# Ten first products from a constant, a pair copy and the placing of blocks off GpSimd, and the constants by two transfers

## The reference, cut to what matters

```python
# x [32, 32, 256], subjects [32] of 8, bias [8, 32], cond weights [8, 32, 32]
h = einsum('bct,bcd->bdt', x, weights[subjects]) + bias[subjects][:, :, None]
# the FFN runs over the last axis of h (256), hidden size 768; w.astype(float8) is the quantization
gate = silu((h @ q(gate_w)) * gate_scale)
up   = (h @ q(up_w)) * up_scale
out  = x + ((gate * up) @ q(down_w)) * down_scale
```

## Time and profile before

| | |
|---|---|
| median of 3 runs | 49.52 us (49.23 to 49.99) |
| the profiled execution, whole | 49.15 us |
| its span in the profile | 47.4 us |
| TensorE busy | 42.6 us (90%) |
| VectorE busy | 38.1 us (81%) |
| ScalarE busy | 25.2 us (53%) |
| GpSimd busy | 4.4 us (9%) |

### The profile page before, as it was taken

How to read it: one execution, slowest core, us unless ns; L and a number is a source line. 1 busy time by engine, 2 the same in 40 slices (tenths; PEclk the granted TensorE clock), 3 DMA queues, 4 the chain that set the end, 5 groups by cost and what they waited for, 6 DMA issues and landing times.

```text
span 47.4 us, 664 instructions
## 1 busy us (share of the span) xinstructions
PE 42.6 (90%) x201; PEld 33.4 (70%) x201; DVE 38.1 (81%) x70; ACT 25.2 (53%) x43; POOL 4.4 (9%) x13
## 2 busy tenths in 40 slices
PE   1999899999999999999999999999999999999000
PEld 1332498798788888888888888887888898987000
DVE  2838899998999999999999999958455569995900
ACT  3734257847519895988695609046554647430000
POOL 3028585200000000000000000000000000000000
PEclk9999999999999999999999999999999999999998
DMA  0398999999990000000000000000000000034392
GB/s 0 99 341 306 353 373 395 404 407 412 417 384 21 0 0 0 14 0 0 0 0 0 0 7 0 0 0 0 0 0 0 0 0 0 7 133 189 121 347 96
DMA packets 2851, 5.71 MB, mean 121 GB/s; under 512 B 288, under 2 KB 928, under 8 KB 2848
## 3 DMA queue, kind: packets, MB, share of 16 engines
q1 hardware_dynamic: 2704, 5.55, 31.6%
q10 hardware_dynamic: 144, 0.13, 0.8%
HBM read 4.63 MB, written 1.05 MB: 120 GB/s over the span
## 4 chain that ended last, share of the span: by engine, by line
PE 73%; DVE 10%; DMA 5%; POOL 2%; issue 2%; ACT 1%; DVEq 1%; POOLq 0%
PE gu L505 46%; PE acc L513 23%; DVE tree_sb L373 6%; DMA const_in<-in_consts_dram 5%; PE acc L478 4%; DVE res L418 2%; POOL cond_bd L314 2%; ACT tree_sb L223 1%; DVEq L70 1%; DVE cond_bd L380 1%; DVEq L364 0%; DVEq L378 0%; POOLq L312 0%
## 5 line engine op out<-in xcount | busy, mean ns | idle before, releaser
L505 PE MATMUL gu<-h_hi,w_q 128*128 128x512 f32 (+1 forms) x52 | 15.0, 376 | 0.0
L505 PE MATMUL gu<-h_lo,w_q 128*128 128x512 f32 (+1 forms) x52 | 14.9, 374 | 0.0
L260 ACT CAST f_hi<-fuse 128x512 fp32r<-128x512 f32 (+1 forms) x13 | 7.6, 588 | 8.8 <-DVE fuse L405 8.6
L505 PEld LDWEIGHTS gu<-h_hi,w_q 128*128 128x128 f32 x52 | 9.5, 188 | 1.9
L505 PEld LDWEIGHTS gu<-h_lo,w_q 128*128 128x128 f32 x52 | 9.5, 188 | 1.8
L405 DVE SCALAR_TENSOR_TENSOR fuse<-gu,const_in,silu 128x512 f32<-128x512 f32 (+1 forms) x13 | 9.2, 706 | 1.5 <-PE gu L505 1.1
L253 ACT ACTIVATE silu<-gu,const_in 128x512 f32<-128x512 f32 (+1 forms) x13 | 8.5, 654 | 3.3 <-PE gu L505 3.3
L413 DVE TENSOR_TENSOR f_lo<-fuse,f_hi 128x512 fp32r<-128x512 f32 (+1 forms) x13 | 8.3, 646 | 2.1 <-ACT f_hi L260 2.1
L513 PE MATMUL acc<-f_lo,w_q 128*128 128x512 f32 (+1 forms) x26 | 8.3, 378 | 0.0
L513 PE MATMUL acc<-f_hi,w_q 128*128 128x512 f32 (+1 forms) x26 | 8.2, 374 | 0.0
L335 DVE SCALAR_TENSOR_TENSOR w_q<-w_big,w_in 128x768 fp32r<-128x768 f32 (+2 forms) x8 | 6.0, 754 | 0.1
(11 more groups left out here) (28 smaller groups left out, 15.9 us busy)
## 6 DMA issues: line engine op xcount, KB each, us to landing
w_in<-in_weights_dram SPq DMA_DIRECT2D x4, 384.0 KB, 6.0
x_tok<-in_x_by_time_dram SPq DMA_DIRECT2D x1, 1024.0 KB, 8.7
out_dram<-res SPq DMA_DIRECT2D x3, 256.0 KB, 2.0
x_sb<-in_x_dram SPq DMA_DIRECT2D x1, 512.0 KB, 3.6
w_in<-in_weights_dram SPq DMA_DIRECT2D x2, 256.0 KB, 4.5
x_sb<-in_x_dram SPq DMA_DIRECT2D x2, 256.0 KB, 4.7
w_in<-in_weights_dram SPq DMA_DIRECT2D x2, 128.0 KB, 5.0
const_in<-in_consts_dram SPq DMA_DIRECT2D x1, 171.0 KB, 2.3
```

Source lines behind the costliest of these rows:

```text
L260: nc.scalar.copy(f_hi[:, s % SLOTS, cols], fuse[:, s % SLOTS, cols]).then_inc(f_hi_made, 1)
L505: last = nc.tensor.matmul(gu[:, (s + q) % 2, part, cols], w_q[:, i, col:col + P], h[:, n, k, cols], start=(v == 0 and k == 0), stop=(v == ...
```

## The change

Four edits. TensorE's first products read a constant of ones in bf16 that the program makes for itself ahead of the kernel's block, broadcast along both dimensions, in place of `warm`; they wait for nothing, there are ten of them and not nine, and VectorE's memset L338 is gone. The copy of the fourth pair of half 0 goes from GpSimd to VectorE, behind the bits and ahead of `select(0)`. The placing goes off GpSimd: in both halves ScalarE places j = 0 and 1, and VectorE j = 2 and 3; GpSimd keeps only the bias work, with both `bias_tok` products in a row. And `const_in` comes by two transfers of 64 partitions each, the first issued by SP as its first, the second by ScalarE ahead of its table load, both counting on `const_ld`, for which everyone now waits to reach 32.

```diff
--- before.py
+++ after.py
@@ -9,7 +9,6 @@
 F32 = mybir.dt.float32
 F32R = mybir.dt.float32r
 I32 = mybir.dt.int32
-U32 = mybir.dt.uint32
 
 P = 128
 
@@ -42,7 +41,7 @@
 
     LAST = 2
     LO_ROW = 32
-    WARM = 9
+    WARM = 10
 
     PIECES = [slice(q * TOK // LAST, (q + 1) * TOK // LAST) for q in range(LAST)]
 
@@ -90,7 +89,6 @@
         w_q = sb("w_q", [P, IC, WCOL], F32R)
         bit_of = sb("bit_of", [P, BITS], I32)
         iota_p = sb("iota_p", [P, 1])
-        warm = sb("warm", [P, P], BF16)
         ones_f = sb("ones_f", [P, P])
         ones_r = sb("ones_r", [P, P], F32R)
         pick_b = sb("pick_b", [P, B])
@@ -111,6 +109,7 @@
         gu = ps("gu", [P, 2, 2, 512])
 
         warm_ps = gu[:, 0, 0]
+        ones_b = nc.const_aps.tensor(1.0, [P, TOK], BF16)
         tree = [tree_sb[:, n].rearrange("p (q g d) -> p q g d", g=GH, d=D) for n in range(HALVES)]
         bits_ps = gu[:, 0, 1, 0:BITS * G].bitcast(I32).rearrange("p (k g) -> p k g", g=G)
 
@@ -119,7 +118,6 @@
         x_ld = [[sem("x_ld0")], [sem(f"x_ld1_{k}") for k in range(KC)]]
         w_ld = [sem(f"w_ld{i}") for i in range(IC)]
         w_down_ld = [sem(f"w_down_ld{i}") for i in range(2)]
-        warm_set = sem("warm_set")
         iota_made = sem("iota_made")
         ones_set = sem("ones_set")
         bit_set = sem("bit_set")
@@ -127,7 +125,7 @@
         bits_made = sem("bits_made")
         bias_pick_made = sem("bias_pick_made")
         tree_even = [sem(f"tree_even{n}") for n in range(HALVES)]
-        tree_even_pool = sem("tree_even_pool")
+        tree_even_dve = sem("tree_even_dve")
         tree_level = [sem(f"tree_level{n}") for n in range(HALVES)]
         cond_placed = [sem(f"cond_placed{n}") for n in range(HALVES)]
         bias_hi_made = sem("bias_hi_made")
@@ -157,9 +155,7 @@
 
         QUANT = ((0, 0, GU), (1, 0, GU), (0, GU, WCOL), (2, 0, WCOL), (1, GU, WCOL)) + tuple((i, 0, WCOL) for i in range(3, IC))
 
-        ACT_BLOCKS = ((0,), (0,))
-        POOL_BLOCKS = ((1,), (1, 2))
-        DVE_BLOCKS = ((2, 3), (3,))
+        ACT_BLOCKS, DVE_BLOCKS = (0, 1), (2, 3)
 
         def wait_quant(eng, i, lo):
 
@@ -184,7 +180,7 @@
             def load_w(i):
                 sp.dma_start(w_in[:, i], weights[i]).then_inc(w_ld[i], 16)
 
-            sp.dma_start(const_in[:], consts).then_inc(const_ld, 16)
+            sp.dma_start(const_in[0:P // 2], consts[0:P // 2]).then_inc(const_ld, 16)
             sp.dma_start(x_sb[:, 0], x[0].rearrange("k p g t -> p k g t")).then_inc(x_ld[0][0], 16)
             load_gate_up(0)
             load_x(0)
@@ -217,9 +213,10 @@
                 act.wait_ge(w_down_ld[i] if lo == GU else w_ld[i], 16)
                 nc.scalar.activation(w_big[:, i, lo:hi], w_in[:, i, lo:hi], ACT.Abs, scale=SHIFT).then_inc(quant_big, 1)
 
+            act.dma_start(const_in[P // 2:P], consts[P // 2:P]).then_inc(const_ld, 16)
             nc.scalar.preload_act_table(ACT.Silu)
 
-            act.wait_ge(const_ld, 16)
+            act.wait_ge(const_ld, 32)
             nc.scalar.copy(tree[0][:, 0:PAIRS - 1], cond_rep[:, 0:PAIRS - 1, 0].unsqueeze(2).to_broadcast([P, PAIRS - 1, GH, D])
                            ).then_inc(tree_even[0], 1)
             nc.scalar.copy(tree[1], cond_rep[:, :, 0].unsqueeze(2).to_broadcast([P, PAIRS, GH, D])
@@ -227,7 +224,7 @@
 
             def place(n):
                 act.wait_ge(tree_level[n], BITS)
-                for j in ACT_BLOCKS[n]:
+                for j in ACT_BLOCKS:
                     nc.scalar.copy(*block_of(n, j)).then_inc(cond_placed[n], 1)
 
             def high_of_h(n, k):
@@ -285,12 +282,6 @@
                            allow_small_or_imprecise_dtypes=True).then_inc(iota_made, 1)
             pool.wait_ge(iota_made, 2)
 
-
-            pool.wait_ge(const_ld, 16)
-            nc.gpsimd.tensor_copy(tree[0][:, PAIRS - 1], cond_rep[:, PAIRS - 1, 0].unsqueeze(1).to_broadcast([P, GH, D])
-                                  ).then_inc(tree_even_pool, 1)
-            pool.wait_ge(tree_even_pool, 1)
-
             def place_bias(n):
 
                 batches = slice(n * TOK // D, (n + 1) * TOK // D)
@@ -307,19 +298,7 @@
             pool.wait_ge(bias_lo_made, 1)
             place_bias(0)
 
-            def place(n):
-
-                pool.wait_ge(tree_level[n], BITS)
-                for j in POOL_BLOCKS[n]:
-                    nc.gpsimd.tensor_copy(*block_of(n, j)).then_inc(cond_placed[n], 1)
-                pool.wait_ge(cond_placed[n], J)
-
-            pool.wait_ge(bd_zeroed, 1)
-            pool.wait_ge(bias_placed, 1)
-            place(0)
             place_bias(1)
-            pool.wait_ge(bias_placed, 2)
-            place(1)
 
         @block.vector
         def _(dve):
@@ -335,7 +314,6 @@
                 nc.vector.scalar_tensor_tensor(w_q[:, i, lo:hi], w_big[:, i, lo:hi], LEAST, w_in[:, i, lo:hi],
                                                ALU.max, ALU.subtract).then_inc(quant_made, 1)
 
-            nc.vector.memset(warm[:].bitcast(U32), 0).then_inc(warm_set, 1)
             nc.vector.memset(ones_f[:], 1.0).then_inc(ones_set, 1)
             for k in range(BITS):
                 nc.vector.memset(bit_of[:, k:k + 1], 1 << k).then_inc(bit_set, 1)
@@ -345,7 +323,7 @@
 
 
 
-            dve.wait_ge(const_ld, 16)
+            dve.wait_ge(const_ld, 32)
             nc.vector.tensor_copy(bias_r[:], bias_in).then_inc(bias_hi_made, 1)
             dve.wait_ge(iota_made, 2)
             nc.vector.tensor_tensor(pick_b[:], subj_all, iota_p[:].to_broadcast([P, B]), ALU.is_equal).then_inc(bias_pick_made, 1)
@@ -353,6 +331,8 @@
             nc.vector.tensor_tensor(bits_ps, subj_own.unsqueeze(1).to_broadcast([P, BITS, G]),
                                     bit_of[:].unsqueeze(2).to_broadcast([P, BITS, G]),
                                     ALU.bitwise_and).then_inc(bits_made, 1)
+            nc.vector.tensor_copy(tree[0][:, PAIRS - 1], cond_rep[:, PAIRS - 1, 0].unsqueeze(1).to_broadcast([P, GH, D])
+                                  ).then_inc(tree_even_dve, 1)
 
             def select(n):
 
@@ -361,7 +341,7 @@
                     left = PAIRS >> k
                     if k == 0:
                         dve.wait_ge(tree_even[n], 1)
-                        dve.wait_ge(tree_even_pool, 1)
+                        dve.wait_ge(tree_even_dve, 1)
                         to = tree[n]
                         data = cond_rep[:, :, 1].unsqueeze(2).to_broadcast([P, PAIRS, GH, D])
                     else:
@@ -372,12 +352,15 @@
                     mask = bits_ps[:, k, groups].unsqueeze(1).unsqueeze(3).to_broadcast([P, left, GH, D])
                     nc.vector.copy_predicated(to, mask, data).then_inc(tree_level[n], 1)
 
+            def place(n):
+                dve.wait_ge(tree_level[n], BITS)
+                for j in DVE_BLOCKS:
+                    nc.vector.tensor_copy(*block_of(n, j)).then_inc(cond_placed[n], 1)
+
+            dve.wait_ge(bd_zeroed, 1)
             dve.wait_ge(bits_made, 1)
             select(0)
-            dve.wait_ge(bd_zeroed, 1)
-            dve.wait_ge(tree_level[0], BITS)
-            for j in DVE_BLOCKS[0]:
-                nc.vector.tensor_copy(*block_of(0, j)).then_inc(cond_placed[0], 1)
+            place(0)
             select(1)
 
             def rest_of_h(n, k):
@@ -385,9 +368,7 @@
                 nc.vector.tensor_tensor(h_lo[:, n, k], acc[:, KC * n + k], h_hi[:, n, k].bitcast(F32),
                                         ALU.subtract).then_inc(h_lo_made, 1)
 
-            dve.wait_ge(tree_level[1], BITS)
-            for j in DVE_BLOCKS[1]:
-                nc.vector.tensor_copy(*block_of(1, j)).then_inc(cond_placed[1], 1)
+            place(1)
             rest_of_w(0)
             round_w(0)
             for n in range(HALVES):
@@ -459,7 +440,7 @@
         def _(pe):
             def keep_warm(count):
                 for _ in range(count):
-                    nc.tensor.matmul(warm_ps, warm[:], warm[:].unsqueeze(1).to_broadcast([P, TOK // P, P]), start=True, stop=True)
+                    nc.tensor.matmul(warm_ps, ones_b[:, 0:P], ones_b, start=True, stop=True)
 
             def bias_of(n):
 
@@ -480,7 +461,6 @@
                                                 start=False, stop=(g == GH - 1), skip_group_check=True)
                     last.then_inc(h_made, 1)
 
-            pe.wait_ge(warm_set, 1)
             keep_warm(WARM)
             for n in range(HALVES):
                 bias_of(n)
```

## The result

The changed kernel took 50.14 us (median of 4 runs, 49.59 to 51.72) where the kernel before took 49.47 in the same series (4 runs, 49.23 to 49.99): a ratio of 1.0134, with a 95% interval of 1.0094 to 1.0175. In a second series, beside 29 runs of the kernel before, it was 1.0138 (1.0089 to 1.0186). So it is slower by 0.7 us, which is under 2 per cent, with an interval that leaves out no change, where 0.37 us less was forecast. The ratios leave out executions more than 1.5 per cent above the fastest of the same kernel, the medians don't.

A forecast was written before the change was run, and what follows sets the result against it. A prologue until 8.61 us, then TensorE alone, bound the kernel, so only an earlier `condition(1)` pays. 0.02 + 0.35 = 0.37 us off 49.52 gave 49.15, called 49.1 us (forecast 48.9 to 49.3, chance 0.48); range 48.5 to 49.8.

The forecast's parts named there:

- What bounds the kernel: Whole chain: prologue until 8.61 us, then TensorE alone; the change gains only what lets TensorE start `condition(1)` earlier.
- The constants by two transfers: Load of the constants at the start: 0.1 us earlier, bounds 0.3 earlier and 0.2 later.
- The rival of the late constants: Start of the kernel: constants don't come earlier, 0.2 us later even, giving 49.3 to 49.45 us; chance 0.12.
- The pair copy on VectorE: VectorE ahead of `select(0)`: a copy of 0.22 us makes the select 0.06 later, at most 0.15.
- Placing half 0: Blocks for `condition(0)`: all four there at 5.81 us where it was 5.82, so no gain.
- the rival that I gave 0.15: Placing half 0: GpSimd's bias work blocks VectorE's placing copies, blocks 0.43 us later, run 49.6 us; chance 0.15.
- Ten first products: TensorE's start: products begin near 0.80 us, end at 5.07, and `condition(0)` starts 0.02 earlier, at 6.10.
- Placing half 1: Ahead of `condition(1)`: blocks complete by 7.93 us, TensorE asks at 8.34, the whole hole goes, 0.35 us earlier.
- Does VectorE keep up: VectorE after the placing: it holds at no cost; tightest at the down columns' rounding, 0.33 us to spare, 0.23 after.
- one of the signs of being wrong: TensorE's later steps: the forecast is wrong if the hole stays or TensorE waits at the down product of step 4.
- The earlier level as the faster rival: TensorE's first products: 2.4 GHz level rises earlier and more evenly, median 48.8 us, or 48.3 with early constants; chance 0.17.
- The late level as the slower rival: TensorE's conditioning passes: level rises later, each microsecond past 6.1 costs 0.5, giving 50.05 or 50.85 us; chance 0.08.

The follow-up runs named there:

- both edits undone: Changed kernel with the constants by one transfer again and GpSimd's bias of half 1 waiting for half 0's placed blocks: 49.11 us, ratio 0.9976; repeated, 49.04 us, 0.9964.

## Why the prediction was wrong, step by step

*What bounds the kernel:* right. The time followed the start of `condition(1)` to within 0.15 us.

*The constants by two transfers:* this is the step that failed. It was put at 0.1 us earlier with 0.2 later as the bound; it came 0.9 later in the profiled execution, and 0.3 to 1.8 later in others. The bound was drawn from one transfer's 2.33 us and a 128-partition store's 2.0, on the tacit assumption that 64 partitions go like 128. Halves of 64 are issued in 0.54 to 0.57 us and not in 0.38, and even with nothing beside them they land after 2.64. The rival of the late constants had the sign, and the same bound of 0.2. Undoing the step brings the changed kernel from 1.0138 to 1.0038. The Trainium skill's rule that I weighed there (DMA: Bandwidth & Descriptors, Issuing engines are not separate DMA queues) says that engines that issue together save only the issue time. Its 0 was nearer than my 0.1 earlier, and the runs go beyond it: SP's second issue began at 1.33 and not 1.17, so issue time was lost, not saved.

*The pair copy on VectorE:* right. 0.22 us, and the select began 0.72 behind the first read of the constants where it was 0.60, so 0.12 late and not 0.06, within the 0.15 that I had allowed.

*Placing half 0:* failed twice. ScalarE's two copies were put at 0.51 us, ending at 5.81; they take 0.62 in every profile that has them, ended at 6.04 with both edits undone, and are the last of the four blocks there. And the rival that I gave 0.15 came true: VectorE's copy waited for GpSimd's bias product. I had priced it at 0.43; it cost VectorE 0.38 and, since ScalarE is late anyway, TensorE 0.18. The evidence that I held against it was weak. The copy at 5.60 inside GpSimd's copy of 5.41 to 5.72 is 0.12 us of overlap on an engine whose recorded spans are rough, and the predicated copies are no test of a plain one: they took 0.73 to 0.74 beside both bias products in the changed kernel too. The row that should have weighed more was GpSimd's 0.67 us copy beside VectorE's L329. The Trainium skill (SBUF — State Buffer, Who interferes with whom) says that the one that starts first keeps the ports for its whole length, and the trace of the changed kernel agrees: 0.60 us with the end 0.09 behind GpSimd's.

*Ten first products:* right as to their times (0.77 to 5.0), and worth nothing, as the summand 0.02 said.

*Placing half 1:* right. The hole is gone in every version that takes this placing off GpSimd, the blocks being there in time (with x late in one of them, for another reason).

*Does VectorE keep up:* nearly. The three low parts' idle time of 0.48 was absorbed: L308 starts at 9.27 (+1.56), the four low parts take 2.48 in one piece, and L308 behind them starts at 13.00, so 1.07 later than the 11.93 of the kernel before. That is 0.23 more than TensorE's delay of 0.84, for VectorE loses the whole 0.38 of its blocked copy and TensorE 0.18. The room of 0.33 shrinks to 0.10, and the down products of step 4 (the fifth), named as the place to look, took 0.05 longer. TensorE's weight load for them waited for VectorE's rounding, which was one of the signs of being wrong:

```profile
22.28 0.30 PEld L493 LDWEIGHTS acc<-f_hi,w_q 128*128 128x128 f32 x2 [0.19 <-DVE w_q L314]
```

With both edits undone no such wait is named. Along the rest another 0.1 was lost in pieces too small to name.

*The earlier level as the faster rival:* its premise, that the kernel before spreads by when the level rises, isn't borne out: its spans stay within 47.4 to 47.6 while its times spread.

*The late level as the slower rival:* the effect is real, its mechanism was another. The level doesn't only rise late; it fell again where late constants left TensorE idle for 2.55 and 2.79 us, and then cost 1.3 and 1.05 us in the 16 passes. I had treated the transfer's delay and the clock as two independent cases; they are one.

## What to carry to other kernels

Before a load at the head of the chain is cut into pieces, look at what kind of piece the trace has timed: a cut by partitions and a cut by columns behaved differently here, and neither beat the one transfer. When a wait is removed together with the work that made it necessary, ask what now runs beside what: GpSimd's bias product had been kept away from VectorE's copies only by a wait that looked like bookkeeping, and putting that one line back was worth 0.34 us. Price such a delay at the engine that waits for it, and not on the engine that suffers it: 0.38 us of VectorE were 0.18 of TensorE, because another engine was nearly as late. And an edit at the start should be judged by ten runs, not three, when it touches a transfer: the changed kernel's own runs span 2.1 us. The span beside each time tells whether a difference is in the kernel's instructions at all.

## What the runs showed of the hardware that I had not expected

A transfer of 64 partitions of 1368 bytes took 0.54 to 0.57 us to issue, on SP and ScalarE together and on SP alone, and the one of x right behind it 0.57 to 0.58; x took 0.40 to 0.44 elsewhere. 128 partitions took 0.37 to 0.43, whole rows or half rows. One transfer on ScalarE's queue with x issued at the same moment on SP's landed after 4.51 us, against 2.33 for the same one ahead of x on SP's queue. VectorE's copy, 0.22 us when free, is recorded as 0.60 when it waits for GpSimd: the wait stands inside the busy time, and the chain calls it "issue". The level of TensorE's clock was up at the bias pair in some profiles (pairs of 0.70 us at 5.01, 5.36, 5.76 and 5.94) and not in others (1.16 at 5.01, 1.19 at 5.08 and 5.29), with the same ten products in front; two of these, both at 5.01, are of one kernel.
